# State-space mixer: front made in blocks of 512 tokens beside the scan, convolution as shifted products, decay factors in PSUM

## What is computed

```python
xr = x @ in_proj_w                       # 128 -> 2 x 256
xi, res = xr[..., :256], xr[..., 256:]
xi = silu(causal depthwise conv of xi, 4 taps, + conv_b)
x_dbl = xi @ x_proj_w                    # 8 (delta) + 16 (B) + 16 (C)
dt = softplus(delta @ dt_proj_w + dt_proj_b)
# scan over tokens, 16 states n per channel, A = -exp(A_log)
states = states * exp(dt * A) + dt * B * xi
y = sum_n states * C
y = (y + xi * Dparam) * silu(res)
out = y @ out_proj_w                     # added to the residual, x is layer-normed before
```

## Time and profile before

| | |
|---|---|
| median of 3 runs | 3420.16 us |
| profiled execution | 3422.07 us, span 3420.8 us |
| granted PE clock, mean over the span | 0.913 |
| PE, DVE, ACT, POOL busy over the span | 3016.5, 2664.0, 2024.8, 925.0 us |
| the mixer, from 2194.8 us to 2612.3 us of the span | 417.5 us |
| of it: layer norm; front; loop with its ends | 10.5; 86.2; 320.8 us |

### The profile page before, as it was taken

One profiled execution on the slowest core, in us unless ns is written; L12 is line 12 of the kernel. 1 busy time (PEld: TensorE's weight loads), 2 busy tenths in 40 slices (PEclk: granted clock), 3 DMA queues, 4 the chain that ended last, 5 costly groups with the idle time before them and its releaser, 6 DMA issues. The chain is left out here.

```text
span 3420.8 us, 59248 instructions
## 1 busy us (share of the span) xinstructions
PE 3016.5 (88%) x23828; PEld 1418.3 (41%) x23828; DVE 2664.0 (78%) x3339; ACT 2024.8 (59%) x3741; POOL 925.0 (27%) x953
## 2 busy tenths in 40 slices
PE   5999999889998699999989999756666977999879
PEld 1222222256666122222235666412223543767745
DVE  7999999656666899999965666779896565888554
ACT  4999999655554599999955555443331235444022
POOL 0000000123332000000012333437673610766400
PEclk7999999989999799999988999868787987999779
DMA  2000000000000100000000000000000000000000
GB/s 91 11 20 14 16 15 15 9 1 1 2 2 1 56 15 15 15 16 15 15 12 1 2 1 2 24 0 0 0 0 9 1 0 0 1 1 1 1 1 13
DMA packets 30221, 35.43 MB, mean 10 GB/s; under 512 B 13623, under 2 KB 24058, under 8 KB 29690
## 3 DMA queue, kind: packets, MB, share of 16 engines
q1 hardware_dynamic: 29754, 31.57, 3.1%
q10 hardware_dynamic: 192, 0.07, 0.0%
HBM read 19.16 MB, written 7.34 MB: 8 GB/s over the span
## 5 line engine op out<-in xcount | busy, mean ns | idle before, releaser
L420 DVE TENSOR_REDUCE max_parts<-banks 128x2 f32<-128x1024 f32 x1024 | 1169.1, 1217 | 19.7 <-PE banks L308 19.2
L510 ACT ACTIVATE probs<-banks 128x512 f32<-128x512 f32 x2048 | 1082.5, 599 | 74.0 <-PE banks L315 57.0
L308 PE MATMUL banks<-k_parts,q_parts 48*128 48x512 bf16 x2048 | 621.4, 396 | 49.6 <-DMA k_parts<-k_scratch 25.4
L315 PE MATMUL banks<-q_parts,k_parts 51*128 51x512 bf16 x2048 | 654.9, 386 | 6.7
L333 PE MATMUL banks<-probs,v_heads 128*9 128x256 f32 x8192 | 637.6, 383 | 7.5 <-ACT pv_copy L521 0.3
L315 PEld LDWEIGHTS banks<-q_parts,k_parts 51*128 51x128 bf16 x2048 | 148.0, 94 | 482.8 <-ACT probs L510 417.6
L550 POOL CAST neg_max_parts<-neg_max 128x8 bf16<-128x8 f32 x64 | 12.9, 201 | 1152.3 <-DVE neg_max L425 1152.3
L333 PEld LDWEIGHTS banks<-probs,v_heads 128*9 128x9 f32 x8192 | 123.7, 88 | 378.9 <-issue 340.2
L1478 PE MATMUL banks<-decay,ident 128*128 128x512 f32 x256 | 158.6, 767 | 103.3 <-POOL decay L1444 103.3
L1444 POOL TENSOR_TENSOR decay<-state,c_row 128x1024 f32<-128x1024 f32 x64 | 212.1, 3336 | 78.8 <-DVE state L1507 78.8
L1507 DVE TENSOR_TENSOR_SCAN state<-decay,state_carry,state 128x1024 f32<-128x1024 f32 x64 | 208.5, 3296 | 0.0
(11 more groups left out here) (428 smaller groups left out, 5332.4 us busy)
## 6 DMA issues: line engine op xcount, KB each, us to landing
outT_half<-pv_copy SPq DMA_DIRECT2D x252, 16.0 KB
prob_sums<-pv_copy SPq DMA_DIRECT2D x252, 2.0 KB
q_scratch<-qk_parts SPq DMA_DIRECT2D x8, 384.0 KB, 3.9
k_scratch<-qk_parts SPq DMA_DIRECT2D x8, 384.0 KB, 2.5
k_parts<-k_scratch SPq DMA_DIRECT2D x32, 96.0 KB
q_parts<-q_scratch SPq DMA_DIRECT2D x28, 96.0 KB
k_parts<-k_scratch SPq DMA_DIRECT2D x32, 64.0 KB
q_parts<-neg_max_rows SPq DMA_DIRECT2D x128, 3.0 KB
```

Source lines behind the costliest of these rows:

```text
L308: nc.tensor.matmul(Mb[m % 2][:, blk(x)], Q[p % 2][half_of(x, ROWS), tile(t)], K[p % 2][half_of(x, ROWS), blk(b)], start=True, stop=True).t ...
L315: nc.tensor.matmul(bank("exp", n, x)[:, :], K[p % 2][half_of(x, ROWS + PARTS), tile(t)], Q[p % 2][half_of(x, ROWS + PARTS), blk(j)], start ...
L420: nc.vector.tensor_reduce(mxp[s % 2][:, :, u // NB, u % NB], Mb[m % 2].rearrange("p (x k) -> p x k", x=2), AX.X, ALU.max).then_inc(*maxed. ...
L510: nc.scalar.activation(PT[:, n % RING, x, :], bank("exp", n, x)[:, :], ACT.Exp, scale=float(HD) ** -0.5).then_inc(*exped.inc())
```

## The change

The three stages become one.

- Entry: `LayerNorm` runs inside `mamba`, interleaved; only block 0 of the front is made before the loop. ACT puts the convolution weights on diagonals, PE spreads them, DVE multiplies them into `in_proj` (`taps`); PE does the convolution as four fp32 matmuls per half and block, each with its tap's weights and the normed input shifted by 0 to 3 tokens, accumulated in a bank. ACT reads it out with the bias.
- The loop has 64 units of 512 tokens: four blocks, 16 states n each. DVE's product and POOL's product take both halves in one instruction of 1024 elements; the scans are two of 512.
- The decay factors go to three PSUM banks in turn; the scan reads them there. POOL's product goes to a buffer `G` of its own. B has one bank, C one, y two, and the front and the output projection share the last one, in a fixed order of uses (`Ring`).
- During block b, the front of block b+1 is made by fixed places n in the unit order, on PE, ACT and POOL; the softplus differences that DVE made are made by POOL for blocks 1 to 3. The projection out, gate and residual of block b-1 also run during block b.
- `sel` is made by a POOL copy from a small matrix; the columns of `x_proj` are rolled on the way in, so that B and C come first.

```diff
+OUT_AT = 11
...
+        xi, res = sb("conv_out", [128, 2, N]), sb("silu_res", [128, 2, N])
         dt, dtx = sb("dt", [128, 2, N]), sb("dt_x", [128, 2, N])
...
-        mamba_front(g, w, res, xi, dt, dtx, BC, sel, negA)
-
...
+        taps, ones = sb("conv_taps", [128, 2, CONV, 128]), sb("ones_square", [128, 128])
+        BC, pick, sel = sb("bc_parts", [96, N], BF16), sb("row_pick", [96, 2 * NS], BF16), sb("row_select", [96, 2 * NS, 128], BF16)
+        bcf, mid, dlt = sb("bc_full", [32, 512]), sb("bc_mid", [32, 512]), sb("delta", [RANK, 512])
+        ee, uu, lu = sb("exp_abs", [128, 2, 512]), sb("one_plus_e", [128, 2, 512]), sb("log_part", [128, 2, 512])
+        negA, carry = sb("neg_A", [128, 2, NS]), sb("state_carry", [128, 2, NS])
+        F, G = two("state", [128, 2, 512]), two("state_times_c", [128, 2, 512])
+        diagonal = G[0][:, :, :].rearrange("p c (q k) -> p c q k", q=CONV)
+        Cs, y = two("c_row", [128, 512]), two("scan_out", [128, 2, 512])
+        norm = LayerNorm(g, mem, g.ps[3:7])
+        Eb, Bb, Cb, Yb = g.ps[0:3], g.ps[3], g.ps[4], g.ps[5:7]
+        decay_bank = lambda m, c: Eb[(2 * m + c) % 3]
...
+            def rests(b):
+                pool.wait_ge(u_back, b + 1)
+                nc.gpsimd.tensor_tensor(ee[:, :, :], uu[:, :, :], ee[:, :, :], ALU.subtract).then_inc(*rests_made.inc())
+                pool.wait_ge(rests_made, b + 1)
+                nc.gpsimd.tensor_tensor(lu[:, :, :], lu[:, :, :], ee[:, :, :], ALU.subtract).then_inc(*logs_made.inc())
+
+            def finish_dt(b):
+                pool.wait_ge(logs_made, b + 1)
+                pool.wait_ge(dt_read, 4 * b + 4)
+                nc.gpsimd.tensor_tensor(dt[:, :, blk(b)], dt[:, :, blk(b)], lu[:, :, :], ALU.add).then_inc(*dt_made.inc())
+                pool.wait_ge(dt_made, b + 1)
+                pool.wait_ge(silued, 2 * b + 1)
+                nc.gpsimd.tensor_tensor(dtx[:, :, blk(b)], dt[:, :, blk(b)], xi[:, :, blk(b)], ALU.mult).then_inc(*dtx_made.inc())
...
+            def times_c(m):
+                pool.wait_ge(scanned, 2 * m + 2)
+                pool.wait_ge(summed, 2 * (m - 1))
...
+            split_rest(0)
+            split_low(0)
+            for m in range(M):
+                b, n = m // NS, m % NS
+                times_c(m)
+                if b > 0 and n == 4:
+                    gate(b - 1)
+                if b + 1 < NB:
+                    if n == 6:
+                        split_rest(b + 1)
+                    if n == 8:
+                        split_low(b + 1)
+                    if n == 12:
+                        rests(b + 1)
+                    if n == 13:
+                        finish_dt(b + 1)
+            gate(NB - 1)
...
+            def convolve(b, c):
+                u = f"v{c}"
+                pe.wait_ge(taps_made, 2)
+                pe.wait_ge(norm.copied, b + 1)
+                pe.wait_ge(*before(u, b))
+                for q in reversed(range(CONV)):
+                    first = max(0, CONV - 1 - q - b * 512)
+                    at = b * 512 + first - (CONV - 1 - q)
+                    i = nc.tensor.matmul(bank(u, b)[:, first:512], taps[:, c, q, :], g.xnT[:, at:at + 512 - first], start=(q == CONV - 1), stop=(q == 0),
+                                         skip_group_check=(b == 0))
+                i.then_inc(*conv_made.inc())
...
+            def spread_b(m):
+                pe.wait_ge(bc_low, m // NS + 1)
+                pe.wait_ge(mid_made, m // NS + 1)
+                pe.wait_ge(b_times_x, m)
+                nc.tensor.matmul(Bb[:, :], sel[:, m % NS, :], BC[:, unit_blk(m)], start=True, stop=True).then_inc(*b_spread.inc())
+
+            def spread_c(m):
+                pe.wait_ge(c_copied, m)
+                nc.tensor.matmul(Cb[:, :], sel[:, NS + m % NS, :], BC[:, unit_blk(m)], start=True, stop=True).then_inc(*c_spread.inc())
+
+            def sum_states(m):
+                n = m % NS
+                pe.wait_ge(c_times_state, m + 1)
+                pe.wait_ge(y_made, 2 * (m // NS))
+                for c in range(2):
+                    nc.tensor.matmul(Yb[c][:, :], g.ident[:, :], G[m % 2][:, c, :], start=(n == 0), stop=(n == NS - 1)).then_inc(*summed.inc())
...
+            spread_b(0)
+            spread_c(0)
+            for m in range(M):
+                b, n = m // NS, m % NS
+                if m + 1 < M:
+                    spread_b(m + 1)
+                    spread_c(m + 1)
+                if b + 1 < NB:
+                    if n in (0, 1):
+                        convolve(b + 1, n)
+                    if n in (2, 3):
+                        project(b + 1, n)
+                    if n == 6:
+                        rows(b + 1)
+                    if n in (8, 10):
+                        project_dt(b + 1, (n - 8) // 2)
+                if b > 0 and n == OUT_AT:
+                    project_out(b - 1)
+                sum_states(m)
+            project_out(NB - 1)
...
+            def times_b(m):
+                dve.wait_ge(b_spread, m + 1)
+                dve.wait_ge(dtx_made, m // NS + 1)
+                dve.wait_ge(c_times_state, m - 1)
+                dve.wait_ge(carried, m - 1)
+                nc.vector.tensor_tensor(F[m % 2][:, :, :], dtx[:, :, unit_blk(m)], Bb[:, :].unsqueeze(1).broadcast_to([128, 2, 512]),
+                                        ALU.mult).then_inc(*b_times_x.inc())
...
+            def scan(m):
+                n = m % NS
+                dve.wait_ge(zeroed, 2)
+                dve.wait_ge(b_times_x, m + 1)
+                dve.wait_ge(carried, m - NS + 1)
...
+                    dve.wait_ge(decay_made, 2 * m + c + 1)
+                    f = F[m % 2][:, c, :]
+                    nc.vector.tensor_tensor_scan(f, decay_bank(m, c)[:, :], f, carry[:, c, n:n + 1], ALU.mult, ALU.add).then_inc(*scanned.inc())
...
+            first_dt()
+            for m in range(M):
+                b, n = m // NS, m % NS
+                times_b(m)
+                scan(m)
+                if b > 0 and n == 1:
+                    finish(b - 1)
+                if b > 0 and n == OUT_AT + 2:
+                    add_x(b - 1)
+            finish(NB - 1)
+            add_x(NB - 1)
...
+            def decay(m):
+                act.wait_ge(A_negated, 1)
+                act.wait_ge(dt_made, m // NS + 1)
+                act.wait_ge(read_out, 4)
                 for c in range(2):
...
+                    act.wait_ge(scanned, 2 * m + c - 2)
+                    nc.scalar.activation(decay_bank(m, c)[:, :], dt[:, c, unit_blk(m)], ACT.Exp, scale=negA[:, c, m % NS:m % NS + 1]).then_inc(*decay_made.inc())
...
             def keep_last(m):
+                act.wait_ge(scanned, 2 * m + 2)
+                nc.scalar.copy(carry[:, :, m % NS], F[m % 2][:, :, 511]).then_inc(*carried.inc())
...
+            norm.deviation(0)
+            norm.copy(0)
+            norm.deviation(1)
+            nc.scalar.preload_act_table(ACT.Silu)
+            read_conv(0, 0)
+            norm.copy(1)
+            read_conv(0, 1)
+            silu_conv(0)
+            nc.scalar.preload_act_table_set("natural_log_exp_and_others")
+            norm.deviation(2)
+            copy_rows(0)
+            norm.copy(2)
+            norm.deviation(3)
+            read_dt(0, 0)
+            read_dt(0, 1)
+            exponential(0)
+            logarithm(0)
+            split_mid(0)
+            norm.copy(3)
+            split_low(0)
+            read_in(0, 2)
+            read_in(0, 3)
+            decay(0)
+            copy_c(0)
+            for m in range(M):
+                b, n = m // NS, m % NS
+                if m + 1 < M and n + 1 < NS:
+                    decay(m + 1)
+                    copy_c(m + 1)
+                if b + 1 < NB:
+                    if n in (0, 1):
+                        read_conv(b + 1, n)
+                    if n in (2, 3):
+                        read_in(b + 1, n)
+                    if n == 4:
+                        nc.scalar.preload_act_table(ACT.Silu)
+                        if b == 0:
+                            silu_res(0)
+                        silu_conv(b + 1)
+                        silu_res(b + 1)
+                        nc.scalar.preload_act_table_set("natural_log_exp_and_others")
+                    if n == 6:
+                        copy_rows(b + 1)
+                    if n == 8:
+                        split_mid(b + 1)
+                    if n == 9:
+                        split_low(b + 1)
+                    if n in (9, 10):
+                        read_dt(b + 1, n - 9)
+                    if n == 10:
+                        exponential(b + 1)
+                    if n == 11:
+                        logarithm(b + 1)
+                if m + 1 < M and n + 1 == NS:
+                    decay(m + 1)
+                    copy_c(m + 1)
+                keep_last(m)
...
-    layer_norm_T(g)
-    g.rest(mixer_in)
-    mamba(g, views(mixer_w, MAMBA_COLS))
```

(48 more changed lines are left out.)

386 lines of the change are left out of this document (148 added, 238 removed).

## The result

The changed kernel takes 3382.86 us (median of 4 runs, 3382.16 to 3389.81) beside 3419.51 us before: ratio 0.9899, 95% interval 0.9881 to 0.9916, so 36.7 us less. Forecast were 3369 and a range of 3338 to 3405. The sign and the range held; the gain is 14 us smaller than the 51 forecast. The profiled execution of the changed kernel took 3389.81 us (span 3388.6), 7 us above its median, where the profiled execution before lay 1.9 us above its own (of three runs), so parts read from its trace add up to somewhat more than the median does.

A forecast was written before the change was run, and what follows sets the result against it. Bound taken: scan and POOL product exclude each other, 8.9 us a unit of 1024 tokens. Loop and end 3.7 + 264.0 + 39.5 + 10 + 11.7 = 328.9 against 317.1, entry gaining 63.3: 3420.2 - 51.5 = 3369 us, range 3338 to 3405.

The forecast's parts named there:

- step 1: In the loop, a scan with its decay in PSUM no longer excludes POOL's product; a scan of 512 takes 1.17 us.
- Rival A: In the loop, a scan with its decay in PSUM still excludes POOL: 4.68 us a unit, 3425 us; chance 0.07.
- step 2: In the loop, scan, POOL product, sum, spread and DVE product form a ring: 8.37 us for two units, 264.0 in all.
- half the idle gap: In the loop, PE idles 1.9 us a unit, against 3.71 us before a slow burst in the old kernel.
- rival B: In the loop, PE's clock stays low at 1.2 GHz, a unit takes 5.13 us: 3443 us, slower; chance 0.06.
- step 4: In the loop, PE's clock falls seldom, at n=4, n=12 to 14 and the start: 10 us.
- The end: From the last scan through product, sum, `finish`, gate, output projection and add: 11.7 us, against 23 before.
- step 3: Front work beside blocks 0 to 2 adds what exceeds each engine's gap: 12.2 us in each, 39.5 with block 3's 2.9.
- waits for `finish`: At the start of blocks 1 to 3, the first sum waits for the previous block's `finish`: 3.2 us late.
- The total: Whole kernel: loop and end 12 us longer, front 63.3 us shorter, net -51.5, so 3369 us.
- step 5: From stage start to the loop's first product: 37 us (34 to 43) instead of 100.3, a gain of 63.3.
- No other stage moved: Sign expected in the profile after: the stages outside the mixer stay unmoved.

The follow-up runs named there:

- number 2: The changed kernel with its three decay buffers in SBUF instead of PSUM: 3419.3 us, ratio 1.0004 to the kernel before.
- number 6: The changed kernel with the four softplus products of blocks 1 to 3 done by DVE instead of POOL: 3389.9 us, ratio 0.9911 to the kernel before.
- number 3: The changed kernel with six zero matmuls before the sum in units without much front work on PE: 3363.5 us, ratio 0.9832 to the kernel before.
- number 4: The changed kernel without the front of blocks 1 to 3, every block scanning block 0 again: 3369.9 us, ratio 0.985 to the kernel before.
- number 5: The changed kernel with `finish` of the previous block after unit n=0 instead of n=1: 3376.1 us, ratio 0.9868 to the kernel before.
- number 1: The changed kernel with PE issuing the spreads of B and C for unit m+2 ahead of the sum of unit m: 3355.1 us, ratio 0.981.
- 11: The changed kernel with early spreads, ACT's readings of PE's results one unit later, and convolutions and following front steps moved: 3322.4 us, ratio 0.972.

## Why the prediction was right, and where it wasn't

**The exclusion goes (step 1): right.** The scan is 1271 ns, not 2.2 us; number 2 puts the PSUM placement at 36 us, as much as the whole gain (the clock's share in it included), and number 6 brings the exclusion back by another door. Rival A is out.

**The ring (step 2): right in its links and its price, wrong in its rhythm.** 8.44 us a pair at the high level where 8.37 stood. What failed is "In the ring PE has 1.9 us free a unit": dividing the pair's time by two. Nothing holds the second unit of a pair back, so both run together and the slack is one gap of 3.86 us. That is no smaller than the 3.70 before the change, so "half the idle gap", which the prediction holds against rival B, was wrong.

**PE's clock (step 4): the term that was mis-sized.** It said "PE idles 1.9 us a unit, so I expect few falls" and took 10 us. In six pairs of block 3 PE idles 3.1 to 5.4 us at a stretch and the sum behind takes 3.2 to 3.7 us; number 3 gives 19.4 us back, where the term held 10. This is rival B on part of the sums. The prediction also read "the slow burst of six records" from a row that the end of its window cuts off; in the trace the burst has eight. The end is late for the same reason: 14.2 us (measured) for 11.7, its sum 3.55 us and its projection 3.49, where the two projections before it took 1.95 and 2.09:

```profile
2571.64 3.55 PE L1565 MATMUL banks<-state_times_c,ident 128*128 128x512 f32 x4 [3.11 <-POOL state_times_c L1492]
...
2579.11 3.49 PE L1572 MATMUL banks<-mixer_weights,scan_out 128*128 128x128 f32 x16 [3.91 <-POOL scan_out L1498]
```

The Trainium skill ("TensorE: Matmul & The Clock Gate", A second HAM failure mode), named beside rival B, reports a clock that oscillates where PE idles briefly between groups of matmuls. This trace agrees in kind: in block 3 the level goes down and up once in most pairs, with sums of 3.68 and 1.88 us in turn.

**Front work (step 3): too high.** Without the waits for `finish`, 31 of its 39.5 us are left, and 13 were measured (number 4). The insertions were priced against a ring at the high level. In truth the loop without them runs mostly at 10.1 us a pair, so part of them fits into gaps that were longer than thought. Part of what they cost may also come back as clock, since PE has more to do: the weight loads of the sums mean 221, 225 and 234 ns in blocks 0 to 2, against 238 in block 3 and 239 in number 4, by an estimate worth some 7 us of sums. How the rest divides wasn't measured.

**The total: right in part by luck.** The errors have opposite signs. The loop without front work is 322 us long (2227.35 to 2549.7 in number 4), where the terms gave 3.7 + 264.0 + 8.7 + 10 = 286: 36 too few. The front beside it costs 14 us in the profiled executions, where the terms gave 31: 16 too many. With 2 to 3 us too few at the end and 1 too many at the entry, the mixer is 21 us longer than forecast in the profiled execution. Of these, 5 are its distance from the median beyond the 1.9 us before, and 1.6 are a gain in other stages; that leaves the miss of 14. The wait for `finish`, priced at 3.2 us a block, is confirmed by number 5: 3.4, 2.4 and 3.5 us at the three block starts.

**Entry (step 5): right,** 36.0 for 37. **No other stage moved:** 30.6 of 32.2 us of the spans' difference lie in the mixer.

What stays open: how much of the 80 us of a front block in number 1 is ACT's work and how much its waits. Numbers 1 and 11 show that 33 us went with the moved reads and front steps, and ACT's waits for PE's results fell by as much; the rest wasn't taken apart. No run spaced the units of a pair evenly, so that it is the bunching that lowers the clock, and not the total idle time of PE, is argued and not shown. The table loads were not tried by themselves.

## What to carry to other kernels

When a shared resource no longer sets the pace, write down the ring that comes next in each engine's list order, and don't spread its slack evenly: with two buffers the units bunched here in pairs, and PE's idle time came in one gap of 3.86 us, behind which the clock was low. When the clock sets the pace, even zero matmuls in the gap paid (number 3). Issue what only waits for a buffer (here the spreads) ahead of what waits for the far end of the pipeline, and read a result out of PSUM one step after asking for it, so that an in-order engine never stands in a wait with urgent work behind it. Before work is moved to a faster engine, see whether its operands put it back into the exclusion.

## What the runs showed of the hardware

A DVE scan with one operand in PSUM isn't held by POOL (1270 or 1271 ns mean in all such runs), with both in SBUF it is (1731 ns); so is a DVE product with two SBUF operands (3.25 us beside a POOL product that took 3.29, against 1.22 and 2.35 alone). ACT's decay of 512 columns takes 688 ns to PSUM and 719 to SBUF in the same places. Adding 1.2 us of zero matmuls in the gaps of units with little front work made the kernel 19 us faster. In block 3 of the changed kernel a sum was at the low level after 3.86 us of idle PE, and with the zeros one was at the high level after 1.11; but one was also at the high level after 3.07 (number 3) and after 3.70.
